# Inputs loaded in stages, and the adding of the expert sums merged with the third layer norm

## The chip, the cores and the metric

One core of one Trainium2 chip runs the whole program. The core has five engines: PE (matrix products), DVE (vector), ACT (activations), POOL (GpSimd) and SP, which in this kernel only issues DMAs. The metric is the device time of one execution in microseconds; before the change the median of three runs is 1676.23 us (1675.97 to 1676.25). All times inside an execution are counted from the start of the span.

## What is computed

Sixteen samples of 548 tokens each (36 image patches and 512 text tokens, 8768 tokens in all) with 128 features go through two transformer layers:

```python
h = concat([patches @ tok_w + tok_b, txt])                   # 16 x (36 + 512) x 128
h = h + gated_attention(layernorm(h))                        # 1: rope on the scores, relu squared
h = h + moe_32_experts(layernorm(h))                         # 2: each expert takes its top 274 tokens, results scattered and added
h = h + spiking_attention(layernorm(h))                      # 3: spikes floor(clip(x, 0, 4) + 0.5), batch norm over all tokens
h = h + swiglu_experts(layernorm(h))                         # 4
```

Each layer norm subtracts the mean over the 128 features and divides by sqrt(variance + 1e-5).

## The kernel before

**Layout and stages.** The hidden state H lies in SBUF for the whole kernel, features on the 128 partitions and the 8768 tokens along the free axis (padded to 8832). Work is cut into blocks. In a block each engine runs a list of instructions in the order in which the source writes them, and waits on semaphores; between two blocks all engines meet at a barrier, so a block ends with its slowest engine and nothing of the next block starts before that. The blocks that the change touches are `load_inputs`, `layernorm` (the first one), `add_rows`, `spike_norm` (the third layer norm) and the start of `project_qkv`.

**load_inputs.** SP issues one DMA for the bias rows, one for the image patches, one for the token weights and one for all the text (L283 to L286), then three small DMAs that write the bias parts to DRAM (L290), waits until these have landed, and issues three that read them back as single rows into `down_b3` (L294). It then waits for all of these, for the image and for the text. ACT issues fifteen DMAs of constants (L302), waits for all of them, and later moves the embedding from PSUM to H (L307). PE waits for both image DMAs and then does 12 products (24 matmul instructions, L316).

**layernorm.** Four sets of four samples. PE subtracts the mean by a product with `center` for each half sample of 274 tokens (L136), ACT copies the result out of PSUM, ACT or POOL squares it, PE sums the squares (L148), ACT takes the root, DVE inverts it and splits it in two parts, PE broadcasts it, DVE scales. Set i consists of the samples i, 4 + i, 8 + i and 12 + i.

**add_rows.** The experts' sums lie in DRAM in two copies. For each of 17 groups of 512 tokens and one of 64, SP loads both copies (L1574, four buffers deep), POOL adds them (L1581), PE transposes four tiles of 128 tokens (L1591), and DVE adds the result to H (L1600). Nothing else runs in this block.

**spike_norm.** The third layer norm, in the same manner as the first, but every set also has four `lift` steps on POOL (L1721) and four `land` steps on DVE (L1756), which make spikes of the scaled values, three scales behind. At its start DVE cuts the projection weights in three bf16 parts (L1761, L1763). PE's order is: all eight halves of set 0, its variance, and then the halves of the next set in turn with the broadcasts of the set before.

```python
            for n in range(8):
                center(0, n)
            variance(0)
            for t in range(sets + 1):
                for n in range(8):
                    if t + 1 < sets:
                        center(t + 1, n)
                    if t >= 1 and (n + 1) * nv % 2 == 0:
                        broadcast(t - 1, (n + 1) * nv // 2 - 1)
                if t + 1 < sets:
                    variance(t + 1)
```

Of the kernel before, what the change touches and what calls it, by code (L numbers as in the profile page):

```python
# [95 lines left out]
def layernorm(nc, k, H, XN, variants, tag, gain=None):  # L96
# [6 lines left out]
    with ExitStack() as st:  # L103
# [156 lines left out]

def load_inputs(nc, x, k, H):

    with ExitStack() as st:
# [4 lines left out]
        parts_d = nc.dram_tensor("bias_parts", [3, BIAS_ROWS, P], BF16, kind="Internal").ap()  # L268
        bias_rest = st.enter_context(nc.sbuf_tensor("bias_rest", [BIAS_ROWS, P], F32))
        bias_part = [st.enter_context(nc.sbuf_tensor(f"bias_part{n}", [BIAS_ROWS, P], BF16)) for n in range(3)]  # L270
        img_in, text_in, const_in, embedded, evacuated, bias_in, cut, laid = (
            sem(n) for n in ("image", "text", "const", "embedded", "evacuated", "bias", "cut", "laid"))
# [4 lines left out]
                  ("ident", "ident"), ("b1_v", "b1_v"), ("W1", "W1"), ("W2", "W2"), ("same_expert", "same_expert"),  # L277
                  ("earlier_group", "earlier_group"), ("router", "router"), ("group_row", "group_row"), ("lanes", "lanes"),
                  ("owner", "owner"), ("odd", "odd")]

        @block.sync
        def _(sp):
            sp.dma_start(bias_rest[:], x["bias_rows"]).then_inc(bias_in, 16)  # L283
            sp.dma_start(patches[:], x["patches"].rearrange("k p n -> p k n")).then_inc(img_in, 16)
            sp.dma_start(tok_w[:], x["tok_w"].rearrange("k p n -> p k n")).then_inc(img_in, 16)
            sp.dma_start(Hb[:, :, PATCHES:S], x["text"]).then_inc(text_in, 16)  # L286

            sp.wait_ge(cut, 6)
            for part in range(3):
                sp.dma_start(parts_d[part], bias_part[part][:]).then_inc(laid, 16)  # L290
            sp.wait_ge(laid, 48)
            for part in range(3):
                r = slice(32 * part, 32 * part + 1)
                sp.dma_start(k["down_b3"][r, :], parts_d[part:part + 1, 0:NE, :].rearrange("o e d -> o (e d)")).then_inc(laid, 16)  # L294
            sp.wait_ge(laid, 96)
            sp.wait_ge(img_in, 32)
            sp.wait_ge(text_in, 16)

        @block.scalar
        def _(act):  # L300
# [3 lines left out]
            at, _ = COLS["tok_b"]  # L304
            for j in range(2):
# [6 lines left out]
        def _(pe):  # L312
            pe.wait_ge(img_in, 32)
            for j in range(2):
                for t in range(TOK_K):
                    last = nc.tensor.matmul(emb[j][:, 0:half], tok_w[:, t, :], patches[:, t, j * half:(j + 1) * half],  # L316
                                            start=t == 0, stop=t == TOK_K - 1)
                last.then_inc(embedded, 1)
# [20 lines left out]
    nc.clear_and_free_semaphores([img_in, text_in, const_in, embedded, evacuated, bias_in, cut, laid])  # L339
# [446 lines left out]
def moe_first(nc, k, x, H, moe_d):  # L786
# [17 lines left out]
    add_rows(nc, k, H, y_d)  # L804
    nc.clear_and_free_semaphores(used)
# [746 lines left out]
def add_rows(nc, k, H, y_d):  # L1552

    with ExitStack() as st:
        sem = lambda n: st.enter_context(nc.semaphore(f"ar_{n}"))
        NBUF, J = 4, 4
        WIDTH = J * P
        rows = [[st.enter_context(nc.sbuf_tensor(f"ar_rows{p}{q}", [P, J, P], F32)) for q in range(2)] for p in range(NBUF)]
        out_ps = [st.enter_context(nc.psum_tensor(f"ar_ps{p}", [P, WIDTH], F32)) for p in range(NBUF)]
        turned, summed, joined = sem("turned"), sem("summed"), sem("joined")  # L1560
        loaded = [sem(f"loaded{p}") for p in range(NBUF)]
        whole = NT // WIDTH
        tail = NT - whole * WIDTH
        groups = [(g * WIDTH, P, J) for g in range(whole)] + [(whole * WIDTH, tail, 1)] * (tail > 0)
        block = st.enter_context(nc.Block())

        @block.sync
        def _(sp):
            for g, (at, r, j) in enumerate(groups):
                p = g % NBUF  # L1570
                if g >= NBUF:
                    sp.wait_ge(turned, g - NBUF + 1)
# [1555 lines left out]
```

## Time and profile before

| what | us |
|---|---|
| median of three runs | 1676.23 |
| the profiled execution, own time | 1674.66 |
| its span, first to last instruction | 1672.8 |
| `load_inputs`, 0 to the first product of the layer norm | 27.7 |
| first layer norm | 67.8 |
| `add_rows` | 34.7 |
| `spike_norm` | 43.1 |
| busy over the whole span: PE, DVE, ACT, POOL | 1300.5, 1036.9, 789.4, 875.4 |

### The profile page before, as it was taken

What the parts mean: (1) busy time and instruction counts of PE and PEld (TensorE: products, weight loads), DVE (VectorE), ACT (ScalarE), POOL (GpSimd) and SP (SyncE); (2) the same over time, 40 slices, a digit from 0 to 9 for tenths busy, and PEclk for the clock granted to TensorE, in tenths of its full rate; (3) what the DMA queues carried; (4) which work ended last, traced back from release to release, by engine and by line L of the source; (5) the groups of instructions that cost most, each with busy time, mean ns of one, the idle gap of its engine ahead of it and who ended that gap; (6) DMA issues with size and microseconds to landing.
All of it is one profiled execution on the core that took longest, in us unless ns stands there. A gap on an engine that the chain in (4) does not pass through costs nothing. (4 is left out here: it accounts for less than half of the span.)

```text
span 1672.8 us, 27218 instructions
## 1 busy us (share of the span) xinstructions
PE 1300.5 (78%) x8667; PEld 915.5 (55%) x8667; DVE 1036.9 (62%) x1943; ACT 789.4 (47%) x1420; POOL 875.4 (52%) x880
## 2 busy tenths in 40 slices
PE   5679999999883430676672883888889888999997
PEld 3567777777652320565561562333333357877775
DVE  2766666666557774211111588888888566667786
ACT  2225454555353330232220454878777657665443
POOL 1455555555331003688885524776776045735766
PEclk8879999999995565899995786999999999999999
DMA  5052000000001031344445200000000311333443
GB/s 181 1 208 114 0 0 0 0 0 0 0 0 28 0 108 28 88 93 83 80 73 154 81 1 2 2 1 0 0 0 1 113 50 55 94 95 46 56 61 40
DMA packets 84627, 81.05 MB, mean 48 GB/s; under 512 B 18330, under 2 KB 73203, under 8 KB 83147
## 3 DMA queue, kind: packets, MB, share of 16 engines
q1 hardware_dynamic: 56205, 59.43, 11.4%
q0 software_dynamic: 26176, 19.40, 8.2%
q10 hardware_dynamic: 2160, 1.13, 0.2%
q8 instruction: 47, 0.77, 0.2%
q14 instruction: 39, 0.31, 0.1%
HBM read 46.36 MB, written 39.64 MB: 51 GB/s over the span
## 5 line engine op out<-in xcount | busy, mean ns | idle before, releaser
L1969 PE MATMUL at_slot<-at_qm,at_ks 128*128 128x512 bf16 (+1 forms) x640 | 160.1, 383 | 19.3 <-DVE at_clip L2174 9.9
L2838 POOL DMA_INDIRECT out_h<-ff_tokens x70 | 109.0, 1557 | 74.7 <-DVE ff_tokens L2891 56.9
L509 PE MATMUL ga_kv<-ga_kern,ga_v 128*128 128x274 f32 x512 | 132.3, 400 | 14.3 <-ACT ga_kern L598 12.8
L2053 ACT ACTIVATE at_clip<-at_slot,at_four 128x1024 bf16<-128x1024 f32 (+1 forms) x96 | 106.8, 1112 | 31.9 <-PE at_slot L1969 30.1
L1452 POOL DMA_INDIRECT moe_sums<-ex_y,slot_sums x69 | 108.3, 1570 | 22.1 <-issue 20.9
L2174 DVE TENSOR_SCALAR at_clip<-at_slot 128x1024 bf16<-128x1024 f32 (+1 forms) x96 | 116.1, 1218 | 3.0 <-PE at_slot L1969 2.6
L509 PEld LDWEIGHTS ga_kv<-ga_kern,ga_v 128*128 128x128 f32 x512 | 92.3, 189 | 37.8 <-ACT ga_kern L598 20.4
L661 POOL TENSOR_TENSOR ga_rot<-ga_by_cos,ga_by_sin 128x274 f32<-128x274 f32 x64 | 48.4, 756 | 114.2 <-DVE ga_by_sin L705 114.1
L590 ACT ACTIVATE ga_rot<-ga_rot 128x274 f32<-128x274 f32 x128 | 55.1, 432 | 109.0 <-POOL ga_rot L661 96.9
L1542 DVE TENSOR_SCALAR ex_share<-ex_rows,owner_sb 128x1 f32<-128x1 f32 x31 | 6.6, 214 | 148.4 <-PE ex_ps_y L1494 148.4
L2828 POOL DMA_INDIRECT by_group<-mx_stage,mx_place_i x69 | 72.0, 1044 | 50.0 <-ACT mx_stage L2714 29.2
L1969 PEld LDWEIGHTS at_slot<-at_qm,at_ks 128*128 128x128 bf16 (+1 forms) x640 | 40.0, 97 | 93.6 <-issue 81.6
L1493 PE MATMUL ex_ps_y<-ex_down,ex_hid 128*128 128x128 f32 (+1 forms) x600 | 86.9, 295 | 3.9 <-ACT ex_hid L1524 3.8
L1436 POOL DMA_INDIRECT ex_rows<-token_rows,slot_tokens x69 | 67.2, 974 | 39.5 <-issue 20.4
L1524 ACT ACTIVATE ex_hid<-ex_ps_up,cols_sb 128x274 f32<-128x274 f32 (+1 forms) x96 | 43.3, 488 | 91.9 <-PE ex_ps_up L1480 91.8
L2110 POOL TENSOR_SCALAR at_qm<-at_qs,at_headmask 128x548 bf16<-128x548 bf16 x120 | 86.3, 738 | 0.0
L1493 PEld LDWEIGHTS ex_ps_y<-ex_down,ex_hid 128*128 128x128 f32 (+1 forms) x600 | 80.6, 204 | 8.2 <-ACT ex_hid L1524 7.0
L1378 POOL DMA_INDIRECT expert_slots<-ct_ids,ct_row x20 | 19.7, 983 | 120.6 <-DVEq L1277 116.0
L2891 DVE SCALAR_TENSOR_TENSOR ff_tokens<-mx_e,ff_tokens 128x128 f32<-128x128 f32 x210 | 72.0, 349 | 15.8 <-ACT ff_tokens L2775 10.8
L2102 POOL TENSOR_SCALAR sa_qkv<-sa_qkv 128x548 f32<-128x548 f32 x48 | 44.5, 927 | 66.5 <-ACT sa_qkv L2065 66.5
L2053 ACT ACTIVATE down_b<-at_slot,at_four 128x1024 bf16<-128x1024 f32 (+1 forms) x48 | 53.4, 1113 | 17.2 <-PE at_slot L1969 16.4
L1518 ACT ACTIVATE ex_xt<-ex_ps_xt 128x256 f32<-128x256 f32 (+1 forms) x32 | 12.7, 396 | 100.6 <-PE ex_ps_xt L1470 100.6
(480 smaller groups left out, 3918.8 us busy)
## 6 DMA issues: line engine op xcount, KB each, us to landing
moe_sums<-ga_zeros SPq DMA_DIRECT2D x8, 1152.0 KB, 13.4
ar_rows<-moe_sums SPq DMA_DIRECT2D x34, 256.0 KB, 3.8
ex_down<-in_down SPq DMA_DIRECT2D x32, 192.0 KB, 2.6
by_group<-in_blank SPq DMA_DIRECT2D x1, 4655.0 KB, 19.8
ff_tokens<-by_group SPq DMA_DIRECT2D x17, 266.0 KB, 3.4
token_rows<-ct_rows SPq DMA_DIRECT2D x17, 256.0 KB, 2.4
out_h<-mx_rows SPq DMA_DIRECT2D x22, 192.0 KB, 2.1
H<-in_text SPq DMA_DIRECT2D x1, 4096.0 KB, 22.1
```

Source lines behind the costliest of these rows:

```text
L509: last = nc.tensor.matmul(kv[:, e, 0:HALF], v[p][:, mt + 2 * side, e * P:(e + 1) * P], kern[(p + g) % 2][:, side, :], start=mt == 0 and si ...
L590: last = nc.scalar.activation(r[:, side], r[:, side], ACT.Relu)
L1436: nc.gpsimd.indirect_dma_start(out=rows[t % NR][:], out_offset=None, in_=rows_d, in_offset=bass.IndirectOffsetOnAxis(ap=gather_idx[:, t:t ...
L1452: nc.gpsimd.indirect_dma_start(out=sums, out_offset=bass.IndirectOffsetOnAxis(ap=scatter_idx[:, t:t + 1], axis=0), in_=y[t % YR][:], in_of ...
L1493: nc.tensor.matmul(out, hid[e % 2][0:m, f, at:at + P], down[e % 2][0:m, f, :], start=opens and f == 0, stop=False)
L1969: last = nc.tensor.matmul(to[r0:r0 + r, g % 2, :].rearrange("p (s n) -> p s n", s=2), ks[m][:, t * P:t * P + r], qm[m][:, 2 * g:2 * g + 2, ...
L2053: nc.scalar.activation(to[0:r], of[0:r], ACT.Relu, bias=four[0:r], scale=-1.0).then_inc(by_act, 1)
L2110: return eng.tensor_scalar(qm[m][:, h, :], qs[:], headmask[:, h:h + 1], 1.0, ALU.mult, ALU.mult)
L2174: nc.vector.tensor_scalar(to[0:r], of[0:r], 4.0, None, ALU.min).then_inc(by_dve, 1)
L2828: nc.gpsimd.indirect_dma_start(out=grouped_d, out_offset=bass.IndirectOffsetOnAxis(ap=place_i[:, t:t + 1], axis=0), in_=stage[:, t, :], in ...
L2838: nc.gpsimd.indirect_dma_start(out=out, out_offset=bass.IndirectOffsetOnAxis(ap=ids, axis=0), in_=R[j % RING], in_offset=None, bounds_chec ...
L2891: nc.vector.scalar_tensor_tensor(r, part(e), share(e), r, ALU.mult, ALU.add).then_inc(acc if e < 3 else weighed, 1)
```

## The change

The attention between the two places, in which DVE adds the bias of the values, is the same before and after. The change has two parts, and some bookkeeping of semaphores and of the buffer `bias_parts`, which are now made once in `build`.

1. `load_inputs`: image and token weights come in three stages of two K tiles each, on semaphores of their own, and PE works stage by stage. The text comes as four DMAs, one for each set of four samples, after the three bias parts in SP's order; its array is laid out for this on the host side. Ten of the fifteen constants move from ACT's queue to the end of SP's. The block no longer waits for text, for these constants or for `down_b3`; the first layer norm does (PE for the text of each set, SP for the rest). ACT does a one-column activation before it waits for the embedding.
2. `add_rows` and `spike_norm` become one block, `sum_and_norm`, written in 25 steps. Step s handles group s of the sums and whatever halves, variance, inversion and scales have come due; a set is now four samples in a row. Turns and centred halves share a ring of three PSUM banks (before: four banks and three banks in the two blocks).

```diff
+        @block.sync                      # in layernorm
+        def _(sp):
+            for part in range(3):
+                r = slice(32 * part, 32 * part + 1)
+                sp.dma_start(k["down_b3"][r, :], k["bias_parts"][part:part + 1, 0:NE, :].rearrange("o e d -> o (e d)")).then_inc(k["late_in"], 16)
+            sp.wait_ge(k["late_in"], 16 * (len(LATE_CONSTS) + 3))
...
+                if n == 0:
+                    pe.wait_ge(k["text_in"][i], 16)
...
+LATE_CONSTS = ("b1_v", "W1", "W2", "same_expert", "earlier_group", "router", "group_row", "lanes", "owner", "odd")
...
             sp.dma_start(bias_rest[:], x["bias_rows"]).then_inc(bias_in, 16)
-            sp.dma_start(patches[:], x["patches"].rearrange("k p n -> p k n")).then_inc(img_in, 16)
-            sp.dma_start(tok_w[:], x["tok_w"].rearrange("k p n -> p k n")).then_inc(img_in, 16)
-            sp.dma_start(Hb[:, :, PATCHES:S], x["text"]).then_inc(text_in, 16)
-
+            for m in range(STAGES):
+                at = slice(m * TOK_K // STAGES, (m + 1) * TOK_K // STAGES)
+                sp.dma_start(patches[:, at], x["patches"][at].rearrange("k p n -> p k n")).then_inc(image_in[m], 16)
+                sp.dma_start(tok_w[:, at], x["tok_w"][at].rearrange("k p n -> p k n")).then_inc(image_in[m], 16)
             sp.wait_ge(cut, 6)
             for part in range(3):
                 sp.dma_start(parts_d[part], bias_part[part][:]).then_inc(laid, 16)
+            for i in range(NGRP):
+                sp.dma_start(H4[:, i, :, PATCHES:S], x["text"][:, i]).then_inc(text_in[i], 16)
+            for name in LATE_CONSTS:
+                sp.dma_start(k[name][:], x[name]).then_inc(late_in, 16)
             sp.wait_ge(laid, 48)
-            for part in range(3):
-                r = slice(32 * part, 32 * part + 1)
-                sp.dma_start(k["down_b3"][r, :], parts_d[part:part + 1, 0:NE, :].rearrange("o e d -> o (e d)")).then_inc(laid, 16)
-            sp.wait_ge(laid, 96)
-            sp.wait_ge(img_in, 32)
-            sp.wait_ge(text_in, 16)
...
+            nc.scalar.activation(warm[:], k["cols"][:, at:at + 1], ACT.Identity, bias=k["cols"][:, at:at + 1])
...
+        NBUF, J, RING = 4, 4, 3
...
+        half_end = [-(-(h + 1) * HALF // WIDTH) for h in range(2 * B)]
+        set_end = [half_end[8 * i + 7] for i in range(sets)]
+        var_step = [e + 1 for e in set_end]
+        invert_step = [e + 2 for e in set_end]
+        scale_step = [[e + 3 + g for g in range(NGRP)] for e in set_end]
+        STEPS = scale_step[-1][-1] + 1
...
+            for s in range(STEPS):                              # PE
+                if s < G:
+                    turn(s)
+                for i, g in scales_at(s):
+                    broadcast(i, g)
+                for i in sets_at(var_step, s):
+                    variance(i)
+                for h in halves_at(s):
+                    center(h)
...
+            pair(0)                                             # POOL
+            for s in range(STEPS + 1):
+                if s + 1 < G:
+                    pair(s + 1)
+                for i in range(sets):
+                    for g in (0, 2):
+                        if half_end[8 * i + 2 * g + 1] == s:
+                            square(i, g)
+                for i, g in scales_at(s - 1):
+                    lift(i, g)
...
+            for s in range(STEPS):                              # DVE
+                if s < G:
+                    add(s)
+                for i in sets_at(invert_step, s):
+                    invert(i)
+                if s == 1:
+                    dve.wait_ge(w_in, 16)
+                if s in (1, 2, 3):
+                    part = s - 1
+                    nc.vector.tensor_copy(w3[:, part, :], w[:]).then_inc(cut, 1)
+                    dve.wait_ge(cut, 2 * part + 1)
+                    nc.vector.tensor_tensor(w[:], w[:], w3[:, part, :], ALU.subtract).then_inc(cut, 1)
+                    dve.wait_ge(cut, 2 * part + 2)
+                for i, g in scales_at(s):
+                    scale(i, g)
+                    n = NGRP * i + g
                     if n >= LAG:
                         land(n - LAG)
```

With this cut the sets end at steps 5, 9, 13 and 18, their variances come at steps 6, 10, 14 and 19, the inversions at 7, 11, 15 and 20, and the scales at 8 to 11, 12 to 15, 16 to 19 and 21 to 24. Comments in this excerpt are added here.

## Rows read from the trace of the kernel before

**Rows 1.** Four stretches: busy time of each engine, granted clock, DMA share, GB/s.
```profile
0.00:27.64 27.64, 7.61 (x24) 5.46 (x24) 5.10 (x16) 2.28 (x3) 0.19 (x4) 0.91 0.82 273
27.64:95.44 67.80, 51.49 (x256) 39.48 (x256) 45.01 (x58) 21.25 (x57) 29.97 (x24) 0.83 0.00 1
899.68:934.34 34.66, 19.26 (x69) 12.35 (x69) 11.81 (x18) 0.00 (x0) 21.91 (x18) 0.50 0.78 259
934.34:977.46 43.12, 36.58 (x192) 25.80 (x192) 31.84 (x52) 19.54 (x53) 21.17 (x24) 0.90 0.02 6
```

**Rows 2.** Timeline of all engines, 20 to 30 us: start, duration, engine, line.
```profile
20.63 0.50 ACT L307 ACTIVATE H<-embedding,cols_sb 128x288 f32<-128x288 f32 x1 [1.07 <-PE embedding L316]
24.83 0.82 SPq L294 DMA_DIRECT2D down_b<-bias_parts  x3
...
27.67 2.62 PE L136 MATMUL ln_centred<-H,center_sb 128*128 128x274 f32 x5 [7.08 <-PEq L263]
```

**Rows 3.** DMA view, issues of the first 70 us: KB each, us to landing.
```profile
H<-in_text SPq DMA_DIRECT2D x1, 4096.0 KB, 22.1
```

**Rows 4.** Timeline of SP's queue, 4 to 5 us.
```profile
4.21 10.70 SPq L290 DMA_DIRECT2D bias_parts<-bias_part  x1
```

**Rows 5.** DMA view, SP's queue from 0 to 14.9 us: packets, MB.
```profile
q1 hardware_dynamic: 2141, 3.25, 66.1%
```

**Rows 6.** DMA view, all queues from 0 to 9.5 us.
```profile
DMA packets 2007, 2.44 MB, mean 257 GB/s; under 512 B 381, under 2 KB 1218, under 8 KB 2007
```

**Rows 7.** DMA view, all queues from 0 to 13 us.
```profile
DMA packets 3354, 3.64 MB, mean 280 GB/s; under 512 B 565, under 2 KB 2261, under 8 KB 3354
```

**Rows 8.** One stretch of four microseconds while the text is read; last figure GB/s.
```profile
16.00:20.00 4.00, 4.00 (x18) 3.14 (x17) 2.04 (x8) 1.78 (x2) 0.00 (x0) 1.00 1.05 384
```

**Rows 9.** Groups of instructions in `add_rows`, by shape.
```profile
L1581 POOL TENSOR_TENSOR ar_rows<-ar_rows 128x512 f32<-128x512 f32 x17 | 21.5, 1265 | 17.1 <-DMA ar_rows<-moe_sums 16.6
L1591 PE MATMUL ar_ps<-ident_sb,ar_rows 128*128 128x128 f32 x68 | 19.0, 435 | 36.8 <-POOL ar_rows L1581 36.8
...
L1600 DVE TENSOR_TENSOR H<-H,ar_ps 128x512 f32<-128x512 f32 x17 | 11.7, 687 | 44.5 <-PE ar_ps L1591 44.5
```

**Rows 10.** Groups of instructions in `spike_norm`, by shape.
```profile
L1721 POOL TENSOR_SCALAR sa_qkv<-sa_qkv 128x548 f32<-128x548 f32 x16 | 12.1, 757 | 8.2 <-DVE sa_qkv L1751 8.2
L1751 DVE SCALAR_TENSOR_TENSOR sa_qkv<-sa_qkv,ln_bcast 128x548 f32<-128x548 f32 x16 | 11.4, 718 | 1.0 <-PE ln_bcast L1678 0.9
...
L1717 POOL TENSOR_TENSOR ln_square<-sa_qkv 128x548 f32<-128x548 f32 x8 | 9.2, 1149 | 14.3 <-ACT sa_qkv L1702 14.3
L1756 DVE TENSOR_SCALAR spikes<-sa_qkv 128x548 bf16<-128x548 f32 x16 | 8.1, 519 | 0.0
...
L1738 DVE RECIPROCAL ln_rstd<-ln_rstd 128x274 f32<-128x274 f32 x4 | 7.5, 1866 | 5.8 <-ACT ln_rstd L1709 5.8
```

**Rows 11.** Timeline of `spike_norm`, one period of a set, and its end.
```profile
954.58 1.57 PE L1665 MATMUL ln_var<-ln_square,mean_rows_sb 128*32 128x274 f32 x16
...
954.79 1.48 POOL L1721 TENSOR_SCALAR sa_qkv<-sa_qkv 128x548 f32<-128x548 f32 x2
955.33 0.44 DVE L1756 TENSOR_SCALAR spikes<-sa_qkv 128x548 bf16<-128x548 f32 x1
...
961.99 1.09 POOL L1717 TENSOR_TENSOR ln_square<-sa_qkv 128x548 f32<-128x548 f32 x1
962.06 1.32 DVE L1756 TENSOR_SCALAR spikes<-sa_qkv 128x548 bf16<-128x548 f32 x1
...
962.36 1.90 PE L1665 MATMUL ln_var<-ln_square,mean_rows_sb 128*32 128x274 f32 x16
...
964.32 0.49 ACT L1709 ACTIVATE ln_rstd<-ln_var,ln_eps 128x274 f32<-128x274 f32 x1 [1.55 <-PE ln_var L1665]
...
975.18 1.94 DVE L1756 TENSOR_SCALAR spikes<-sa_qkv 128x548 bf16<-128x548 f32 x4
```

**Rows 12.** Timeline of PE at the start of `add_rows`.
```profile
904.65 0.69 PE L1591 MATMUL ar_ps<-ident_sb,ar_rows 128*128 128x128 f32 x2 [27.24 <-POOL ar_rows L1581]
```

More of the change, by code:

```diff
@@ L803, in moe_first @@
         run_experts(nc, k, x, gather_idx, scatter_idx, rows_d, y_d, used)
[L804 to L805 removed]
+    return y_d, used
 KEY_LOW = 7
@@ L1565, in add_rows @@
-        block = st.enter_context(nc.Block())
+        rows = [[sb(f"rows{p}{q}", [P, J, P]) for q in range(2)] for p in range(NBUF)]
+        sq = [sb(f"square{g}", [P, S]) for g in range(NGRP)]
+        rstd = sb("rstd", [P, HALF])
+        rstd_parts = [[sb(f"rstd{part}{i}", [P, HALF], F32R) for part in range(2)] for i in range(2)]
+        eps = sb("eps", [P, 1])
+        w = sb("w", [P, 3 * P])
+        ring = [ps(f"ring{j}", [P, 512]) for j in range(RING)]
+        var_ps = ps("var", [P, 512])
@@ new lines, in sum_and_norm @@
+        scale_step = [[e + 3 + g for g in range(NGRP)] for e in set_end]
+        STEPS = scale_step[-1][-1] + 1
+        halves_at = lambda s: [h for h in range(2 * B) if half_end[h] == s]
+        sets_at = lambda steps, s: [i for i in range(sets) if steps[i] == s]
+        scales_at = lambda s: [(i, g) for i in range(sets) for g in range(NGRP) if scale_step[i][g] == s]
+        uses = [use for s in range(STEPS) for use in [("turn", s)] * (s < G) + [("half", h) for h in halves_at(s)]]
+        use_of = {use: n for n, use in enumerate(uses)}
@@ L1567, in _, with tokens, whole @@
+        bank_of = lambda kind, n: ring[use_of[kind, n] % RING]
+        block = st.enter_context(nc.Block())
+        def tokens(t, h):
+            return t[:, h * HALF:(h + 1) * HALF]
+        def whole(t, i, g):
+            at = (i * NGRP + g) * S
+            return t[:, at:at + S]
         @block.sync
@@ L1583, in _, with free_bank @@
         @block.tensor
         def _(pe):
-            for g, (at, r, j) in enumerate(groups):
-                p = g % NBUF
-                pe.wait_ge(joined, g + 1)
-                if g >= NBUF:
-                    pe.wait_ge(summed, g - NBUF + 1)
+            def free_bank(kind, n):
+                last_use = use_of[kind, n] - RING
+                if last_use >= 0 and uses[last_use][0] == "turn":
+                    pe.wait_ge(summed, uses[last_use][1] + 1)
+                elif last_use >= 0:
+                    pe.wait_ge(evacuated, evacuated0 + uses[last_use][1] + 1)
+                return bank_of(kind, n)
@@ L1590, in _, with turn @@
+            def turn(g):
+                at, r, j = groups[g]
+                pe.wait_ge(paired, g + 1)
+                bank = free_bank("turn", g)
                 for t in range(j):
-                    last = nc.tensor.transpose(out_ps[p][:, t * r:(t + 1) * r], rows[p][0][0:r, t, :], k["ident"][0:r, 0:r])
+                    last = nc.tensor.transpose(bank[:, t * r:(t + 1) * r], rows[g % NBUF][0][0:r, t, :], k["ident"][0:r, 0:r])
                 last.then_inc(turned, 1)
-        @block.vector
@@ L1656, in variance, with center @@
+            def center(h):
+                pe.wait_ge(summed, half_end[h])
+                bank = free_bank("half", h)
+                nc.tensor.matmul(bank[:, 0:HALF], k["center"][:], tokens(H, h), start=True, stop=True).then_inc(centred, 1)
             def variance(i):
@@ L1711, in _, with pair @@
         @block.gpsimd
         def _(pool):
+            def pair(g):
+                at, r, j = groups[g]
+                p = g % NBUF
+                pool.wait_ge(loaded[p], 32 * (g // NBUF) + 32)
+                nc.gpsimd.tensor_tensor(rows[p][0][0:r, 0:j], rows[p][0][0:r, 0:j], rows[p][1][0:r, 0:j], ALU.add).then_inc(paired, 1)
             def square(i, g):
```

200 lines of the change are left out of this document (74 added, 126 removed).

## The prediction

> **What bounds the kernel now.** I read the page's span by slices first, then the stretches between barriers, then the timeline of each of the two places that the change touches. No engine bounds the kernel as a whole; at each place something else does. [Rows 1] have the four stretches that count. In the input block (27.64 us) PE works for 7.61 us and DMA is busy for 0.82 of the time. The first layer norm (67.80) has no DMA. `add_rows` (34.66) has POOL at 21.91, PE at 19.26, DVE at 11.81, a granted clock of 0.50, and 259 GB/s. `spike_norm` (43.12) has PE at 36.58, DVE at 31.84, POOL at 21.17, ACT at 19.54 and next to no DMA. So two things wait one after the other that could run together: loading and layer norm at both places. The reader should see that the two last stretches have nearly the same total on POOL (43.1) and DVE (43.7).
>
> The input block ends by SP's list, not by PE. PE starts when the token weights have landed and ends at 20.6, when ACT moves its last result [rows 2]. The text lands 22.1 us after its issue, at 24.3 [rows 3]. SP's first write of a bias part, a DMA of 8 KB, takes 10.70 us to issue [rows 4]; because of this the parts are written late, their reading back is issued at 24.83, and the first product of the layer norm comes at 27.67 [rows 2].
>
> **What held SP's issue.** At 14.9, when that issue ended, SP's queue had moved 2141 packets [rows 5]. Everything issued up to the text is 32 + 768 + 768 + 2048 data packets plus 16 for each of four DMAs, 3680. 
>
> **Part 1, the inputs.** Removed from the block's end: the wait for the text, and the round trip of `down_b3`. Moved past SP: four text DMAs (528 packets each) and ten constants (144 each), after six image DMAs (272 each) and the three parts (48 each).
> - Image: it and five constants are now alone in front, 1824 packets on SP's queue and about 720 on ACT's, 2544 together. Before, 2007 packets had moved by 9.5 and 3354 by 13 [rows 6, 7], 385 per us, so all have moved at 9.5 + 537 / 385 = 10.9. PE has one of three stages left then (7.61 / 3 = 2.5, [rows 1]), ACT two moves of 0.50 [rows 2]: ready at 15. The early activation takes a table load off ACT's path, which costs nothing as PE was busy behind it.
> - Text of set 0, 1 MB at 384 GB/s [rows 8]: 2.7 us later, about 14 to 15. The later sets need it only one set period apart, and each takes 2.7 us: hidden.
> - SP: by the limit the tenth constant can be issued when all but the last 144 + 1539 of 1824 + 2112 + 1440 = 5376 packets have moved, at 3693. That is 1869 packets into the text, at 384 / 2.048 = 188 per us: 9.9 us after 10.9, at 20.8. With an issue and the barrier the first product comes at about 21.6. **The gain is 27.7 - 21.6 = 6.1 us.** Bounds: 5 if the queue holds fewer; without any limit ACT and the text decide, at about 15, a gain of 12.7. I take 6.1 since the one stall of the trace is on this same queue with the same packets.
> - In the layer norm: the wait for each set's text and SP's three small DMAs and its wait for the constants (landed by about 27) lie beside 67.8 us of work: nothing. PE is idle for some 7 us before it, as before, so the clock at its start is the same.
>
> **Part 2, the merged block.** Removed: one barrier, and the two stretches one after the other, 899.68 to 977.46 = 77.8 us. Added: nothing computed. The work of one set of 4.28 groups, by engine:
> - POOL: 4.28 pairs of 1.27, two squares of 1.15, four lifts of 0.76 [rows 9, 10]: 5.4 + 2.3 + 3.0 = 10.7.
> - DVE: 4.28 adds of 0.69, an inversion, four scales of 0.72, four lands of 0.52. The inversion is a reciprocal of 1.87 and a cut of about 0.7: of DVE's 31.84 us in `spike_norm` 4.8 remain after scales, lands and reciprocals, for four such cuts and three of the weights [rows 1, 10]. 2.9 + 2.6 + 2.9 + 2.1 = 10.5.
> - PE: its period in `spike_norm` at full clock is 962.36 - 954.58 = 7.8 [rows 11]; 4.28 x 4 transposes, 0.14 each at full clock if they take half of the 0.28 from start to start at 0.5 (19.0 us for 68, [rows 9]), give 2.4 more: 10.2.
> - DMA: 34.66 - 3.6 for the first load over 18 groups, 1.7 a group: 7.4.
>
> Three engines at 10.2 to 10.7 that hand work to one another in fixed order can't all be full. What queues behind what: a `turn` waits for POOL's `pair` and for a bank that DVE's `add` of the step before gives back; with an inversion DVE holds that up for 2.6 us; a `square` waits for the centring that PE does last in the step, and the next `pair` stands behind it on POOL. `spike_norm` filled PE to 0.85 with one engine as the bound [rows 1]. With three, and with the port below, I take the same share of the longest, 10.7 / 0.86 = 12.4 per set, 2.9 per step. Bounds: 2.5 (POOL without a gap) and 3.6 (an inversion and two squares in full on top: 10.7 + 2.6 + 2.3 = 15.6 a set).
>
> The sum: the first turn comes at 904.65 [rows 12]. Steps 0 to 6 have no scales; PE starts at half clock, where a turn (4 x 0.28) and two centrings (five instructions, two to a centring, span 2.62 in the first layer norm) take about 2.9 [rows 2, 9], and once it is granted full clock POOL and the loads set 1.8 to 2.1; I take 2.2 each, step 7 begins at 920. Eleven steps at 2.9 end at 952. After the last add come centring, square and variance (3.1), the root, then what ran in `spike_norm` from 964.32 to 977.12 [rows 11], less the set before's four scales of 0.72 with a little waiting (3.1): 9.7. End at 952 + 3.1 + 9.7 = 965. **The gain is 977.5 - 965 = 12.5 us,** bounds 5 (3.6 a step) and 17 (2.5 a step), 20 if the first steps run at 1.8 as well. The weights' DMA now stands after one group on SP's queue and costs 0.6 us of it, in the 2.2. ACT (20 us in all) is never late. Releasing the semaphores costs no more than the 0.3 us between the two blocks, which goes.
>
> **A rule and the rows.** When POOL does a square at 961.99, a land of DVE takes 1.32 in place of 0.44 and ends 0.3 after it; during two lifts a land takes 0.44 as ever [rows 11]. The pairs are of the square's kind, so about a third of the lands and casts will wait, some 2 us a set on DVE, which is in the 12.4. The Trainium skill (SBUF — State Buffer, Who interferes with whom) says that a DVE copy, cast or tensor_scalar in its two-port mode and any GpSimd instruction exclude each other for their whole length. The square's row agrees, the lift's row doesn't. Were it so for lifts too, POOL's 43.1 us and some 13 of DVE would exclude each other; the block would be no shorter than 3.6 + 56 + 2 = 62, against my 65, and the fast case below would fall away.
>
> **Rivals.**
> - *A, SP isn't held by the text.* The input block ends at 15: 1676.2 - 12.7 - 12.5 = 1651.0. For it: one stall only, and ACT's fifteen issues showed none. Against: the count above, and the length of that stall. 0.13.
> - *B, the merged block runs at POOL's pace,* 2.5 a step, first steps 1.8: 1676.2 - 6.1 - 20 = 1650.1. For it: POOL has no gaps to fear from loads four deep. Against: the shared ring of three banks. 0.17.
> - *C, lockstep:* 3.6 a step, because inversions and squares each stop all: 1676.2 - 6.1 - 4.5 = 1665.6. Against: scales and pairs of other sets are there to fill. 0.20.
> - *D, slower than before: PE stays at the clock of 0.50.* `add_rows` ran at it throughout [rows 1]. PE would need 19.3 + 36.6 x 0.90 / 0.50 = 85 us, with the first load 90, with idle time at the inversions about 95: 17 more than 77.8, time 1676.2 - 6.1 + 17 = 1687. It decides from 83.9 us on for the block. Against: in `add_rows` PE was 0.56 busy, in `spike_norm` 0.85 and had a mean of 0.90; here it is nearly always busy at half clock. 0.04.
> - *E, no change:* the merged block takes 80 to 87 us and eats what the inputs give, by D's mechanism in part of the block. 0.02.
>
> **How the numbers follow.** My own case has 0.44: 1676.2 - 6.1 - 12.5 = 1657.6. The sums stand against the profiled span of 1672.8 (own time 1674.66); the median is 1.6 above that, and the same difference is assumed after. Range 1647 to 1668: from just under A and B to just over C. It leaves out D, E and A with B together (1643.5), and some of C's far side, under 2 in 10. About 0.2% (3.4 us) is what a measurement of this kernel tells from no change. Faster 0.94 (all but D and E), same 0.02, slower 0.04.
>
> **What would show it.** The first product of the layer norm at 21 to 22, an issue on SP's queue of several us on one of the texts or constants, and the image embedded by 15. The layer norm 67.8 long. The merged block about 65 long, its last add near 952, a granted clock near 0.85, steps with an inversion longer than the rest, lands of over 1 us beside pairs. Wrong would be: a first product at 15 (A), steps of 2.5 (B) or 3.6 (C), a clock of 0.50 in the block (D), or a stage far from both places that moves by more than 2 us, for which I see no reason in the rows.

## The result, and the profile after

The changed kernel took 1656.99 us (median of 4 runs, 1654.36 to 1657.61) beside 1676.10 (4 runs, 1675.84 to 1676.25): a ratio of 0.9883, interval [0.9866, 0.9900]. The profiled execution took 1657.27 (1674.66 before), with a span of 1655.5 beside 1672.8.

Where the time went is read by setting the same instants of the two traces side by side. Each row's figure is the start of an instruction that exists in both kernels.

| From, to | before, us | after, us | gained |
|---|---|---|---|
| start, first product of the first layer norm | 27.7 | 18.8 | 8.9 |
| from there to the start of the gated attention (first layer norm) | 67.8 | 66.5 | 1.3 |
| from there to the first load of the expert sums | 804.3 | 804.8 | -0.5 |
| from there to the projection's first product (the block) | 78.3 | 71.7 | 6.6 |
| from there to the end of the span | 694.8 | 693.7 | 1.1 |
| span | 1672.8 | 1655.5 | 17.3 |

So the total came out as forecast (19.1 by the medians, 17.4 by the two profiled executions, 18.6 forecast), but of the two parts the first gave more than its term (8.9 for 6.1) and the second about half of its own (6.6 for 12.5). The middle and the end move little: in a second trace of the changed kernel (`changed_again`, below) they are 804.4 and 694.4 long.

The stretches that answer to [rows 1]: the input block, the first layer norm, and the merged block in place of the two last ones. Columns: busy time of PE, its weight loads, DVE, ACT and POOL, granted clock, DMA share, GB/s.

```profile
0.00:18.77 18.77, 7.61 (x24) 5.47 (x25) 5.10 (x16) 2.56 (x4) 0.19 (x4) 0.92 0.94 323
18.77:85.25 66.48, 49.73 (x256) 38.38 (x256) 44.69 (x58) 21.14 (x57) 29.96 (x24) 0.84 0.07 23
890.09:961.30 71.21, 48.78 (x261) 35.55 (x261) 47.72 (x70) 20.03 (x53) 42.41 (x42) 0.81 0.42 130
```

In the merged block POOL, DVE and PE are busy for 0.60, 0.67 and 0.69 of the time: the reader should see that none of them fills it.

**The inputs.** Timeline of the changed kernel, 0 to 30 us, answering to [rows 2] and [rows 4]:

```profile
4.26 1.47 SPq L304 DMA_DIRECT2D bias_parts<-bias_part  x3
5.77 3.89 SPq L306 DMA_DIRECT2D H<-in_text  x4
9.70 2.33 SPq L308 DMA_DIRECT2D b_v_sb<-in_b_v  x1
13.18 0.98 ACT L320 ACTIVATE H<-embedding,cols_sb 128x288 f32<-128x288 f32 x2 [4.22 <-PE embedding L330]
17.87 0.43 SPq L308 DMA_DIRECT2D odd_sb<-in_odd  x1
18.80 5.96 PE L145 MATMUL ln_centred<-H,center_sb 128*128 128x274 f32 x16 [5.17 <-PEq L275]
```

ACT has moved the last embedding at 14.16 (13.18 + 0.98), and the parts' issues take 1.47 us in all where the first alone took 10.70 [rows 4]. PE then waits 5.17 us for the barrier, and what the barrier waits for is SP: its last issue, `odd`, ends at 18.30. The DMA view of SP's queue, to 10.9 and to 18.3 us (packets, MB, share of 16 engines), answers to [rows 5]:

```profile
q1 hardware_dynamic: 2058, 2.68, 75.2%
```
```profile
q1 hardware_dynamic: 3507, 5.55, 87.3%
```

At 18.3 there stand 5376 - 144 - 3507 = 1725 packets in front of the last constant. Worked out in the same way at three earlier returns in this run, by 14.69, 15.96 and 17.32, it is 1574, 1607 and 1639; at the first and the third (12.07 and 13.26) it is 1655 and 1702.

**The block.** Its start, then one step with an inversion, then its end. Timeline of the changed kernel, 886 to 963 us; L1652 is `turn`, L1728 `pair`, L1658 `center`, L1734 `square`, L1738 `lift`, L1780 `land`.

```profile
893.59 1.26 POOL L1728 TENSOR_TENSOR ln_rows<-ln_rows 128x512 f32<-128x512 f32 x1 [9.80 <-DMA ln_rows<-moe_sums]
894.90 1.12 PE L1652 MATMUL ln_ring<-ident_sb,ln_rows 128*128 128x128 f32 x4 [27.20 <-POOL ln_rows L1728]
897.43 3.87 POOL L1728 TENSOR_TENSOR ln_rows<-ln_rows 128x512 f32<-128x512 f32 x3 [2.58 <-DMA ln_rows<-moe_sums]
898.74 1.12 PE L1652 MATMUL ln_ring<-ident_sb,ln_rows 128*128 128x128 f32 x4 [2.72 <-POOL ln_rows L1728]
...
925.83 1.10 POOL L1734 TENSOR_TENSOR ln_square<-sa_qkv 128x548 f32<-128x548 f32 x1 [2.07 <-ACT sa_qkv L1702]
926.90 0.65 POOL L1738 TENSOR_SCALAR sa_qkv<-sa_qkv 128x548 f32<-128x548 f32 x1
927.51 1.26 POOL L1728 TENSOR_TENSOR ln_rows<-ln_rows 128x512 f32<-128x512 f32 x1
928.83 0.66 PE L1652 MATMUL ln_ring<-ident_sb,ln_rows 128*128 128x128 f32 x4 [1.64 <-POOL ln_rows L1728]
...
934.31 1.26 POOL L1728 TENSOR_TENSOR ln_rows<-ln_rows 128x512 f32<-128x512 f32 x1
934.60 1.28 DVE L1780 TENSOR_SCALAR spikes<-sa_qkv 128x548 bf16<-128x548 f32 x1
...
946.22 1.86 PE L1658 MATMUL ln_ring<-H,center_sb 128*128 128x274 f32 x4
948.92 2.86 POOL L1738 TENSOR_SCALAR sa_qkv<-sa_qkv 128x548 f32<-128x548 f32 x4
949.27 0.60 DVE L1780 TENSOR_SCALAR spikes<-sa_qkv 128x548 bf16<-128x548 f32 x1
950.98 0.49 ACT L1713 ACTIVATE ln_rstd<-ln_var,ln_eps 128x274 f32<-128x274 f32 x1 [1.20 <-PE ln_var L1669]
959.01 1.95 DVE L1780 TENSOR_SCALAR spikes<-sa_qkv 128x548 bf16<-128x548 f32 x4
961.78 1.55 PE L1847 MATMUL pq_ps<-spikes,w 128*128 x6 [3.53 <-ACTq L1853]
```

Read the four rows from 925.83 as one chain. POOL stood idle 2.07 us for ACT's moves of a centred group, because `square` is in front of the next `pair` in its list. Then square, lift and pair run back to back, and PE's next `turn` comes when the pair is done, after 1.64 us without work. A `turn` is then late because a square in front of its pair waited for the half that was centred last; nothing in the data asks for that.

The chain of waits in the block, sums over it (us in total, times, longest):

```profile
PE ln_ring L1652 <- POOL ln_rows L1728: 35.7, 8, 27.2
DVE H L1757 <- PE ln_ring L1652: 18.8, 11, 5.8
POOL ln_square L1734 <- ACT sa_qkv L1702: 15.8, 8, 3.3
POOL ln_rows L1728 <- DMA ln_rows<-moe_sums: 12.4, 2, 9.8
```

Take PE's 27.2 off as the first load, which began before the block: in the other seven POOL costs PE 8.5 us. The POOL row below it is where that comes from: all eight squares wait for ACT, 15.8 us in all. Loads are late once after the first (2.6), never later.

### The profile page after: what moved, and what is told of

It reads as the page before. It is cut to its first block and busy times, and to the rows that moved or that the text cites. A ratio compares the mean times of both kernels' runs of the same rounds, so it can differ in the third digit from the quotient of the medians.

```text
span 1655.5 us, 27252 instructions
## 1 busy us (share of the span) xinstructions
PE 1294.0 (78%) x8667; PEld 913.6 (55%) x8667; DVE 1040.4 (63%) x1943; ACT 789.0 (48%) x1421; POOL 874.9 (53%) x880
## 3 DMA queue, kind: packets, MB, share of 16 engines
q1 hardware_dynamic: 57757, 60.24, 11.6%
## 5 line engine op out<-in xcount | busy, mean ns | idle before, releaser
L1995 PE MATMUL at_slot<-at_qm,at_ks 128*128 128x512 bf16 (+1 forms) x640 | 161.0, 385 | 19.1 <-DVE at_clip L2200 9.7
L2079 ACT ACTIVATE at_clip<-at_slot,at_four 128x1024 bf16<-128x1024 f32 (+1 forms) x96 | 106.8, 1112 | 33.4 <-PE at_slot L1995 31.5
L752 DVE TENSOR_TENSOR ga_ukv<-ga_kv,ga_u 128x548 f32<-128x548 f32 x32 | 23.3, 729 | 58.2 <-PE ga_kv L505 58.2
```

The source lines that it names most:

```text
L1995: last = nc.tensor.matmul(to[r0:r0 + r, g % 2, :].rearrange("p (s n) -> p s n", s=2), ks[m][:, t * P:t * P + r], qm[m][:, 2 * g:2 * g + 2, ...
L2079: nc.scalar.activation(to[0:r], of[0:r], ACT.Relu, bias=four[0:r], scale=-1.0).then_inc(by_act, 1)
```

## The experiments

Two theories stood after this. *Theory:* the inputs are set by SP's held issues, and the block's steps by POOL's order, squares in front of pairs. *Rivals:* that one part changed what the other gave; that in the block DVE is the bound with its lands stretched by POOL; that PE's clock of 0.50 at its start costs what is missing; that the weights' DMA behind the first group delays all. `in_only`, `merge_only`, `late_in_norm` and `pair_ahead` ran on a chip where the kernel before takes 1761.74 (1757.53 to 1764.8, 10 runs), so their times are compared with that alone; the changed kernel itself did not run there. `changed_again`, `act_squares`, `w_late` and `all_four` stand beside 1675.47 (1674.43 to 1677.94, 7 runs), `parts_first`, `early_products`, `no_land` and `late_squares` beside 1674.93 (1673.86 to 1676.93, 7 runs).

**The parts alone.** `in_only` is the change's first part without the second, `merge_only` the reverse.

> Only part 1 (staged inputs), add_rows and spike_norm as before. Theory by the profile after: the input block ends 8.9 us earlier (first product of the layer norm at 18.8, not 27.7) and nothing else changes by design, so 1676.1 - 8.9 = 1667.2, give or take 1.5 for where the clock's dips fall. Rival, my forecast's account (part 1 gives 6.1): 1670.0. Rival, the two parts depend on one another: any other value.

> Only part 2 (merged block), inputs as before. Theory by the profile after: the stretch from the first load of the sums to the first product of the projection takes 71.7 us and not 78.3, so 1676.1 - 6.6 = 1669.5, give or take 1.5. Rival, my forecast's account (part 2 gives 12.5): 1663.6.

Measured: `in_only` 1753.33 (ratio 0.9950 [0.9932, 0.9968]), 8.4 us less, first product at 18.9, block 78.9. `merge_only` 1754.00 (0.9951 [0.9934, 0.9969]), 7.7 us less, block 69.9. Together 16.1, beside 16.9 for both in one kernel (`changed_again`, on another chip, below): no sign that one part changes what the other gives. By the intervals the second part is worth 5.5 to 11.6 us, which leaves out 12.5. For the first they allow 5.6 to 12.0, so the time doesn't tell 6.1 from 8.9; the instant of the first product does.

**The late constants out of SP's way.**

```diff
 in load_inputs
-            for name in LATE_CONSTS:
-                sp.dma_start(k[name][:], x[name]).then_inc(late_in, 16)
 in layernorm, SP's list
         def _(sp):
+            for name in LATE_CONSTS:
+                sp.dma_start(k[name][:], k["x"][name]).then_inc(k["late_in"], 16)
             for part in range(3):
```

> The changed kernel, with the ten late constants issued by SP at the start of the layer norm's block and not at the end of the input block. Theory: what ends the input block after the change is SP's issuing of these ten, held up behind the text (it ends at 18.3 while ACT's last move ends at 14.2); with them gone the first product comes at 14.7, 4.1 us earlier than 18.8: 1657.0 - 4.1 = 1652.9. Rival: the block then waits for the bias parts to land in DRAM or the layer norm for the first text (issue at 7 plus 7.3 to land), first product at 16 or later, gain under 3. Rival: the issue of the text itself is held, no gain.

Timeline of that run, 12 to 16 us:

```profile
13.69 0.99 ACT L320 ACTIVATE H<-embedding,cols_sb 128x288 f32<-128x288 f32 x2 [4.50 <-PE embedding L330]
14.94 0.35 SPq L133 DMA_DIRECT2D b_v_sb<-in_b_v  x1
14.98 1.39 PE L147 MATMUL ln_centred<-H,center_sb 128*128 128x274 f32 x5 [0.85 <-PEq L277]
```

PE waits 0.85 us, not 5.17: ACT's last move ends at 14.68 and the first product is at 14.98. The whole took 1738.70 (0.9869 [0.984, 0.9899]), an interval that overlaps the changed kernel's own (0.9866 to 0.9900): what the edit is worth is read from the instants and not from the time. So the last 3.8 us of the changed kernel's input block are SP's ten issues and nothing else; the layer norm behind it was 66.35 long, no longer for having them.

**The parts before the text,** in the kernel before, one run.

```diff
-            sp.dma_start(Hb[:, :, PATCHES:S], x["text"]).then_inc(text_in, 16)
-
             sp.wait_ge(cut, 6)
             for part in range(3):
                 sp.dma_start(parts_d[part], bias_part[part][:]).then_inc(laid, 16)
+            sp.dma_start(Hb[:, :, PATCHES:S], x["text"]).then_inc(text_in, 16)
```

> The kernel before, with SP's three writes of the bias parts issued ahead of the text and not behind it. Theory: the first of these issues took 10.7 us because the text in front of it had to be cut into packets first; ahead of the text each takes under 1 us, the round trip of down_b3 is over before the text lands, and the first product comes right after the text, at 25 to 26 in place of 27.7. Rival: something else holds that first issue (what DVE writes, or DRAM as the target), it takes 10 us again, and the first product stays at 27 or later.

SP's timeline in that run:

```profile
4.21 1.34 SPq L288 DMA_DIRECT2D bias_parts<-bias_part  x3
5.59 0.68 SPq L289 DMA_DIRECT2D H<-in_text  x1
13.34 1.91 SPq L293 DMA_DIRECT2D down_b<-bias_parts  x3
```

The same three 8 KB writes take 1.34 us when the text isn't in front of them: what cost 10.70 [rows 4] was the DMA ahead, not the write. The first product came at 25.05, 2.6 earlier, and only that: the text lands at 23.8 now (5.59 + 18.2), and the reads of the parts, issued at 13.34, stand behind it in the queue. Which of the two the block then waits for isn't told apart. The time of this one run was 1673.1, under the lowest of the kernel before (1673.86) by less than a microsecond.

**POOL a pair ahead.**

```diff
             pair(0)
+            pair(1)
             for s in range(STEPS + 1):
-                if s + 1 < G:
-                    pair(s + 1)
+                if s + 2 < G:
+                    pair(s + 2)
```

> The changed kernel with POOL's pair of group s + 2 in step s, not s + 1. Theory: the merged block is slow (3.2 us a step in steps 7 to 17) because on POOL the next pair stands behind a square that waits for the centring done last in PE's step; with the pair one step ahead, PE's turns (8.5 us of waits for POOL) stop waiting, steps go to about 2.8: gain 4 us, 1653.0. Rival: DVE, with its inversions and port waits, sets the step anyway: within 1 us of 1657.0. Rival: loads come too late for the longer lead: slower by 1 to 3 us.

Waits of the block in that run:

```profile
PE ln_ring L1652 <- POOL ln_rows L1728: 27.2, 2, 25.4
POOL ln_square L1734 <- ACT sa_qkv L1702: 10.2, 7, 2.4
```

PE's waits for POOL fall from eight to two, with 1.8 us beside the first load. The block is 67.1 long, steps 7 to 17 take 28.95 (2.9 each; 32.4 in the changed kernel). The time was 1739.99 (0.987 [0.9846, 0.9894]), which again can't be told from the changed kernel's own ratio.

Could a higher clock have made these steps short? Turns 7 to 17 of `late_in_norm`, which has the block as changed, and of `pair_ahead`, on one chip (columns as above; the clock stands third from the end):

```profile
912.73:944.02 31.29, 23.71 (x145) 17.05 (x144) 24.12 (x32) 10.76 (x31) 22.71 (x23) 0.95 0.35 117
917.51:946.46 28.95, 22.55 (x146) 17.27 (x144) 23.81 (x32) 10.76 (x31) 21.25 (x22) 0.94 0.41 126
```

At the same clock the new order is 2.3 us shorter. The clock does have a part: in the traces with POOL's order as changed, ten steps take 31.3 to 31.8 at 0.95 to 0.97 and 32.4 to 33.4 at 0.87 to 0.90, so about 1 us of the changed kernel's 32.4 may be the clock's.

**The squares on ACT.**

```diff
-                if g % 2 == 1:
-                    if i > 0:
-                        act.wait_ge(var_done, var0 + i)
-                    last = nc.scalar.activation(sq[g][:, j * HALF:(j + 1) * HALF], bank[:, 0:HALF], ACT.Square)
+                if i > 0:
+                    act.wait_ge(var_done, var0 + i)
+                last = nc.scalar.activation(sq[g][:, j * HALF:(j + 1) * HALF], bank[:, 0:HALF], ACT.Square)
...
-                for i in range(sets):
-                    for g in (0, 2):
-                        if half_end[8 * i + 2 * g + 1] == s:
-                            square(i, g)
```

The waits of PE and DVE for POOL's squares are gone as well.

> The changed kernel with all squares of the merged block on ACT (from PSUM) and none on POOL. Theory: POOL and its order hold the merged block; the eight squares (9.2 us, and 15.8 us of POOL's waiting for the values ahead of them) go, so the ten steps from turn 7 to turn 17 take 28 us in place of 32.4, the block about 66, the whole 3 to 5 us less than the changed kernel. Rival: DVE sets the step; steps stay at 3.1 to 3.2 and the whole within 1 us.

Its block, and PE's turns 7 and 17:

```profile
889.40:953.30 63.90, 42.28 (x261) 31.22 (x261) 46.30 (x69) 23.82 (x69) 34.25 (x34) 0.87 0.46 144
```
```profile
911.41 0.60 PE L1652 MATMUL ln_ring<-ident_sb,ln_rows 128*128 128x128 f32 x4
...
938.45 0.27 PE L1652 MATMUL ln_ring<-ident_sb,ln_rows 64*128 64x64 f32 x1
```

To the projection's first product, as the other blocks are counted, the block is 64.4 long (63.9 to the start of the next block). Turns 7 to 17 take 27.04 us (2.7 each, at a clock of 1.00; 31.8 at 0.97 in the changed kernel beside it), and the time is 1653.90 (0.9873 [0.9856, 0.9889]), 4.6 less than the changed kernel beside it (`changed_again`); all four runs (up to 1655.3) lie under all four of that (from 1657.55). ACT had the room: 23.82 busy of 63.9.

**The changed kernel again,** on the same chip as `act_squares`.

> The changed kernel itself, to stand beside the others on one chip: 0.9883 of the kernel before, as measured first. The merged block 71.7 us from first load to first product of the projection in the first trace, but 69.9 and 68.6 in two kernels with the same block; theory: this spread is where the dips of the granted clock fall, so this trace lies between 68 and 72 too.

It took 1658.53 (0.9903 [0.9887, 0.992]): first product 19.1, block 71.0, turns 7 to 17 31.8. Its granted clock in two stretches of the block:

```profile
890.30:903.00 12.70, 5.92 (x20) 4.54 (x21) 4.29 (x8) 0.85 (x3) 5.55 (x5) 0.50 0.86 274
903.00:930.00 27.00, 20.64 (x130) 14.30 (x128) 19.12 (x24) 12.19 (x32) 19.85 (x18) 0.98 0.66 197
```

**The weights' DMA behind four groups and not one.**

```diff
-                if g == 1:
+                if g == 4:
                     sp.dma_start(w[:], x["wqkv"]).then_inc(w_in, 16)
...
-                if s == 1:
+                if s == 4:
                     dve.wait_ge(w_in, 16)
-                if s in (1, 2, 3):
-                    part = s - 1
+                if s in (4, 5, 6):
+                    part = s - 4
```

> The changed kernel with the projection weights' load after group 3 and their cutting in steps 4 to 6. Theory: the load in front of group 1 made the second turn come 3.8 us after the first, where add_rows had 1.8; with it moved the second turn comes 1.8 to 2 after the first and the block is up to 2 us shorter. Rival: step 1 to 6 are bound by PE at the low clock and by DVE, the lost start is made up by step 7, nothing gained.

PE's first two turns in that run:

```profile
897.77 1.11 PE L1652 MATMUL ln_ring<-ident_sb,ln_rows 128*128 128x128 f32 x4 [28.31 <-POOL ln_rows L1728]
899.84 1.11 PE L1652 MATMUL ln_ring<-ident_sb,ln_rows 128*128 128x128 f32 x4 [0.96 <-POOL ln_rows L1728]
```

The second turn comes 2.07 us after the first in place of 3.84. But 3.84 is the first trace's alone: with the weights' DMA where the change has it, this gap is 2.3 to 2.9 in seven other traces (2.87 in `changed_again`, 2.32 in `merge_only`) and 4.3 in `early_products`. From the second turn to the eighth it is 13.7 to 13.8 in the block as changed, and 13.7 here. So the edit is worth 0.3 to 0.9 us against most traces. The block is 68.3 long, against 68.6 to 71.7 for the changed one, and the time is 1658.34 (0.989 [0.9873, 0.9906]), that of `changed_again`: that the edit pays is not shown.

**PE kept busy while the first loads run.** Products whose result nothing reads, five ahead of the loop and two after the first turn.

```diff
+            for n in range(5):
+                nc.tensor.matmul(var_ps[:, 0:EXPAND], k["center"][:], k["b1_v"][:], start=True, stop=True)
             for s in range(STEPS):
                 if s < G:
                     turn(s)
+                for n in range(2 if s == 0 else 0):
+                    nc.tensor.matmul(var_ps[:, 0:EXPAND], k["center"][:], k["b1_v"][:], start=True, stop=True)
```

> The changed kernel with five idle products on PE while the first sums load and two after the first turn (their result is never read). Theory: the clock is at 0.50 at the first turns because PE did nothing for 20 us, and with work just before it is granted 1.0 sooner; turns 2 to 6, now 2.5 apart, come 1.8 to 2.1 apart and turn 7 comes 14 to 15 us after the first and not 16.1 to 17.6. Rival: what sets these steps is DVE's cutting of the weights and POOL's pairs; turn 7 stays at 16 or more.

The clock of the first 14 us, and PE's turns:

```profile
889.00:903.00 14.00, 7.88 (x29) 5.91 (x30) 2.42 (x4) 0.40 (x1) 4.88 (x4) 0.74 0.64 207
```
```profile
900.64 0.66 PE L1652 MATMUL ln_ring<-ident_sb,ln_rows 128*128 128x128 f32 x4 [2.79 <-POOL ln_rows L1732]
...
908.09 0.63 PE L1652 MATMUL ln_ring<-ident_sb,ln_rows 128*128 128x128 f32 x4 [1.40 <-DVE H L1761]
```

From the first turn to the eighth the clock was 0.91, where it is 0.76 and 0.74 in the two traces of the changed kernel, and the first two turns took 0.66 for 1.12. Yet turns 0 to 7 took 18.45 us (17.6 and 16.6 there) and the time was 1659.47 (0.9893 [0.9873, 0.9914]). The half clock is there, and taking much of it away gained nothing: the second turn waits for POOL and its load (2.79), the one at 908.09 for DVE's add (1.40). The trace shows what held this add: its turn had ended by 905.8, but DVE's list has a cutting of the weights in front of it, whose subtraction ran to 907.23, and the add began at 907.26.

**No lands,** one run. This leaves out the sixteen thresholds on DVE; the spikes are the constant 1.0.

```diff
+            nc.vector.memset(spikes[:], 1.0)
...
-                    if n >= LAG:
-                        land(n - LAG)
-            for n in range(B - LAG, B):
-                land(n)
```

> The changed kernel without the sixteen lands on DVE (the spikes are a constant 1.0, set while the first sums load), so without 8 us of DVE's work and without the part of it that waits for the port. Theory: POOL's order sets steps 7 to 17, DVE does not; the ten steps from turn 7 to turn 17 stay above 30 us (31.3 to 33.0 in four traces), and only the end after the last add gets shorter, by 2 to 3.5. Rival: DVE and the port set the step; the ten steps fall to 28 or less.

Its waits and turns 7 and 17:

```profile
PE ln_ring L1652 <- POOL ln_rows L1728: 34.6, 8, 27.0
...
POOL ln_square L1734 <- ACT sa_qkv L1702: 18.1, 8, 3.4
```
```profile
912.64 0.60 PE L1652 MATMUL ln_ring<-ident_sb,ln_rows 128*128 128x128 f32 x4
...
945.58 0.37 PE L1652 MATMUL ln_ring<-ident_sb,ln_rows 64*128 64x64 f32 x1
```

With 9.1 us of DVE's work gone, ten steps take 32.9, as with it (32.4), and the waits stand: the lands do not set the steps. That the rest of DVE's work doesn't either is shown by `pair_ahead` and `act_squares`, which shorten the steps and leave DVE's work as it is. From turn 17 to the projection's first product it is 15.4 us, where the traces with the lands and with POOL's squares have 16.0 to 17.5; I had expected more. The time was 1657.34.

What the lands and POOL do to one another can be read from the ends of single instructions. POOL's lifts around two lands, first in the kernel before (the land of 955.33 in [rows 11]), then in the changed one (the land of 949.27 above):

```profile
954.79 0.65 POOL L1721 TENSOR_SCALAR sa_qkv<-sa_qkv 128x548 f32<-128x548 f32 x1
955.50 0.78 POOL L1721 TENSOR_SCALAR sa_qkv<-sa_qkv 128x548 f32<-128x548 f32 x1
...
948.92 0.65 POOL L1738 TENSOR_SCALAR sa_qkv<-sa_qkv 128x548 f32<-128x548 f32 x1
949.54 0.83 POOL L1738 TENSOR_SCALAR sa_qkv<-sa_qkv 128x548 f32<-128x548 f32 x1
```

The land of 949.27 ends at 949.87, 0.30 after the lift that it began beside (948.92 + 0.65), and the land of 934.60 ends 0.3 after its pair (935.57). Every land that began more than 0.2 us before the end of a POOL instruction ended 0.30 or 0.31 us after it, beside lifts, pairs and squares alike, in eleven traces. The land of 955.33 began only 0.11 before the end of its lift and so could still take 0.44. The other way round, a lift that begins during a land takes 0.77 to 0.85 and not 0.65, and ends 0.50 after the land.

**Versions that beat both.** `late_squares` has the late constants out of the way and the squares on ACT; `all_four` also has the pair ahead and the weights' DMA behind four groups.

> The changed kernel with the late constants in the layer norm's block, the weights' load after group 3, the pair two ahead, and the squares on ACT. If the gains add: 4.1 for the inputs, 1 for the weights, 5 for pair and squares together (they remove the same waits), 10 us less than the changed kernel, 0.982 of the kernel before. Rival: DVE's 48 us bound the block, so the last three together give 2 and the whole 6.

> The changed kernel with two edits alone: late constants in the layer norm's block, squares of the merged block on ACT. If these two make up what all four gave: 4 and 5 us, 0.9816 of the kernel before within 0.0015. Rival: the pair two ahead and the later weights add something: 2 us or more above that, 0.983 or higher.

`all_four` took 1645.73 (0.9816 [0.9799, 0.9832]), 12.8 less than the changed kernel on its chip, with a block of 64.7 and ten steps in 28.05; `late_squares`, in the other group of runs, 1647.09 (0.9829 [0.9812, 0.9846]), 65.0 and 27.1. The intervals overlap, so they aren't told apart. With the squares on ACT a pair ahead and the later weights add nothing that shows.

## Why the prediction came out, and where its steps did not

**The total was right because two terms erred in opposite directions:** the inputs by +2.8 and the first layer norm by +1.3, the block by -5.9, the rest by +0.6. That sum is -1.2, against a forecast gain of 18.6 in a span that gave 17.3. It is luck as well that the medians gave 19.1: the forecast took both kernels' medians to stand alike to their profiled executions, but the one before was 1.4 above it and the one after 0.3 below. The steps:

- *The limit on SP's queue.* That SP is held by what stands in front is shown: `parts_first` moves the 10.70 us away by order alone, and `late_in_norm` ends the input block with ACT. Rival A is out. Its size was low: 1725 packets stood at the last return and not 1539. Of the 2.8 us (18.8 for 21.6), 186 packets at the 188 per us used are 1.0, the barrier took 0.47 where I had an issue and a barrier at 0.8, and 234 packets more had moved by 10.9 (2058, not 1824), 1.2 at the same rate: 2.5 together. The rest is the rate itself: the 1449 packets between 10.9 and 18.3 took 7.4 us and not the 7.7 of 188 per us. Which quantity the chip limits (packets, or something that goes with them) isn't shown, since the stand at the returns ranges from 1540 to 1725.
- *Ready at 15.* This held: ACT's last move ended at 14.16, and at 14.68 in `late_in_norm`.
- *The first layer norm at 67.8.* 66.5 here; over the traces it was 65.0 to 68.3 for the same lists on PE, DVE, ACT and POOL, so 1.3 is no effect that these runs can show.
- *The merged block, 65.3 forecast, 71.2 measured: the step that failed.* From three places. Turns 0 to 7: 17.6 for 15.4; from the second turn on they take 13.75 for 13.2, and the first gap is 3.84 for 2.2. That gap is 2.3 to 2.9 in most traces of the same order, so the 0.6 for the weights' DMA was about right, and what made it 3.84 here stays open. Steps from 7 on: 3.24 each to turn 17 and not 2.9, 33.6 for 32 to the last add's end. The end: 15.2 for 12.8, of which 1.75 lies ahead of the last root, where PE does broadcasts of the set before between the last centrings (0.93 and 0.87 us), and 0.6 behind it. The other traces of the same block are up to 3.1 shorter (68.6 to 71.7 to the projection's first product, where the forecast comes to 65.8), so of the 5.9 some 3 to 6 are the forecast's error.
- *What the steps wait for.* The prediction named it (the next `pair` stands behind `square`, which waits for centring) and then priced steps by a share of 0.86 of the longest engine, taken from a stretch with one bound (whose rows give 0.85). `pair_ahead` shows the price: with this queue opened, steps are 2.9, the forecast's own figure. `act_squares` does it by the other end, 2.7.
- *DVE's lands beside POOL.* They do stretch, as the square's row had it in [rows 11]: the land at 934.60 takes 1.28 beside a pair, and the mean is 0.58 for 0.52 in [rows 10], 1.0 us over all sixteen. `no_land` shows that they cost the steps nothing. Where the prediction read [rows 11] as a lift that does not hold a land, the reading was wrong: the land began 0.11 us before the first lift ended, and the second lift took 0.78 for 0.65. The rule of the Trainium skill (SBUF — State Buffer, Who interferes with whom) would have each wait until the other's instruction is over, and these traces agree for lifts as for pairs and squares: a land is done 0.30 us after such an instruction's end. By the prediction's reckoning the block was then to be no shorter than 62, which all these runs keep and none tests.
- *Rival C, 3.6 a step,* was nearer for the block's gain (6.6 for its 4.5) than my own case; the steps (3.24) lie halfway between the two. B would have needed 2.5 a step. *D and E:* the clock of 0.50 was there for the first 13 us of the block, 0.98 in the 27 after them (`changed_again`), 0.81 over the whole block, and no change in the time came of raising it at the start.

**Open:** why the first gap between turns is 2.3 in one trace and 3.84 in another, and what else beside the clock makes one code's block 68.6 to 71.7 long.

## What to carry to other kernels

- When two stretches with different bounds are merged, price the merged step by each engine's list order and not by busy shares: look for a load-side instruction (here `pair`) behind one that waits for a late result (here `square`), and put it one step ahead or give the waiting work to an engine with room.
- Two errors of opposite sign can make a total right; only instants read in both traces tell.

## What the runs showed of the hardware that was not expected

- SP's issues are held by what stands in its queue: 10.70 us for an 8 KB write behind a transfer of 2048 packets [rows 4], 1.34 us for three such writes without it. At the returns 1540 to 1725 packets stood in the queue. ACT's five issues at the start took 0.42 to 0.48 us each.
- A land of DVE and an instruction of POOL, lifts included, shut each other out: a land that meets one ends 0.30 us after it (1.28 long in place of 0.44 beside a pair), and a lift that begins during a land ends 0.50 us after that (0.78 in place of 0.65).
- PE's clock was 0.50 over the block's first 13 us, after 27 us without a product, and 0.98 in the 27 after them. With 0.91 in place of 0.74 over turns 0 to 7, turn 7 came no earlier after the first.
